# One token-tile pipeline of a Mamba layer and a key-routed expert layer: 25 instead of 21 gathered rows per tile weighed by way of TensorE, and another order of stages and row groups

## What is computed

```python
x = layernorm(x + mamba(x))                      # layer 1
h = silu(x @ W_up.T + b_up) @ W_down.T + b_down  # [tokens, 256]
sim = h @ W_q.T ... keys                         # 2 x 8 heads x 64 keys
sc, indices = top8 of the 64 sums of the top8 of each half, per head
de, ue = down_embed[indices], up_embed[indices]  # 64 rows of 256 and of 512 per token
z = silu(einsum('btd,bthkd->bthk', h, de) * softmax(sc))
x = layernorm(x + einsum('bthk,bthkd->btd', z, ue))
```

## Time and profile before

| | |
|---|---|
| time, median of 3 runs | 3131.76 us (3126.43 to 3133.64) |
| the profiled execution's own time | 3120.3 us |
| its span from the first to the last instruction | 3118.5 us |
| granted TensorE clock, mean over the span | 0.931 |
| busy share DVE / PE / ACT / POOL | 89% / 84% / 75% / 66% |
| mean rate of the DMA engines over the span | 275 GB/s |

### The profile page before, as it was taken

One profiled execution on the slowest core, in us unless ns is written; L12 is line 12 of the kernel. 1 busy time (PEld: TensorE's weight loads), 2 busy tenths in 40 slices (PEclk: granted clock), 3 DMA queues, 4 the chain that ended last, 5 costly groups with the idle time before them and its releaser, 6 DMA issues.

```text
span 3118.5 us, 42958 instructions
## 1 busy us (share of the span) xinstructions
PE 2628.5 (84%) x10688; PEld 1613.2 (52%) x10688; DVE 2770.7 (89%) x10160; ACT 2325.9 (75%) x6674; POOL 2062.9 (66%) x2056
## 2 busy tenths in 40 slices
PE   7988888888888888888888888889888888888862
PEld 4455555555555555555555555555555555555531
DVE  3489899989999999999999999999999998999986
ACT  3477887777887777787777788777788777788753
POOL 0067676666676676676667667667667666667676
PEclk9999999999999999999999999999999999999975
DMA  8078888888888888888888888888888888888897
GB/s 284 26 264 279 283 285 268 280 291 279 279 289 273 273 299 280 281 289 269 268 296 281 281 285 282 263 281 294 282 279 289 272 275 292 279 278 290 271 310 271
DMA packets 189850, 856.65 MB, mean 275 GB/s; under 512 B 36192, under 2 KB 39392, under 8 KB 189088
## 3 DMA queue, kind: packets, MB, share of 16 engines
q0 software_dynamic: 163840, 805.44, 77.0%
q1 hardware_dynamic: 19104, 34.87, 3.2%
q10 hardware_dynamic: 6656, 13.60, 1.2%
HBM read 845.38 MB, written 8.39 MB: 274 GB/s over the span
## 4 chain that ended last, share of the span: by engine, by line
DVE 35%; PE 33%; ACT 11%; issue 9%; DMA 6%; POOL 6%; POOLq 0%; ACTq 0%; DVEq 0%; SPq 0%
PE bank L463 15%; DVE ring L1167 9%; DVE bank L1181 9%; PE bank L479 7%; POOL ring L275 6%; DMA ring<-embed,idx 6%; PE bank L338 3%; DVE i L1097 3%; ACT xc L704 3%; DVE v L1091 2%; DVE xdt L1138 2%; ACT scaled L673 2%; PE bank L470 2%; ACT coef L664 2%; DVE place L1124 1%
## 5 line engine op out<-in xcount | busy, mean ns | idle before, releaser
L275 POOL DMA_INDIRECT ring<-embed,idx x2048 | 2061.6, 1007 | 1040.9 <-issue 517.0
L1181 DVE SCALAR_TENSOR_TENSOR bank<-ring,coef,bank 128x512 f32<-128x512 f32 x1312 | 988.0, 753 | 8.8 <-ACT coef L664 1.4
L1167 DVE SCALAR_TENSOR_TENSOR ring<-ring,hcur 128x256 f32<-128x256 f32 x2048 | 815.4, 420 | 58.0 <-DMA ring<-embed,idx 55.7
L664 ACT ACTIVATE coef<-prob,zp 128x1 f32<-128x1 f32 x2048 | 455.6, 293 | 237.0 <-DVE ring L1167 235.8
L463 PE MATMUL bank<-w_up,zs 128*128 128x512 f32 x1024 | 509.4, 650 | 97.5 <-ACT zs L793 93.9
L506 PE MATMUL bank<-cst,scaled 128*128 128x128 f32 x2688 | 410.9, 305 | 171.9 <-ACT scaled L673 171.8
L506 PEld LDWEIGHTS bank<-cst,scaled 128*128 128x128 f32 x2688 | 351.2, 159 | 245.9 <-ACT scaled L673 213.3
L673 ACT ACTIVATE scaled<-ring,coef 128x512 f32<-128x512 f32 x672 | 446.8, 714 | 10.4
L463 PEld LDWEIGHTS bank<-w_up,zs 128*128 128x128 f32 x1024 | 206.6, 210 | 335.4 <-issue 233.9
L1012 DVE SCALAR_TENSOR_TENSOR xc<-raw,taps,xc 128x128 f32<-128x128 f32 x960 | 265.5, 348 | 90.7 <-ACT xc L704 90.6
L338 PE MATMUL bank<-w_in,ut 128*128 128x512 f32 (+1 forms) x768 | 289.7, 528 | 47.1 <-ACT seg L689 47.1
(11 more groups left out here) (150 smaller groups left out, 3764.4 us busy)
## 6 DMA issues: line engine op xcount, KB each, us to landing
ring<-embed,idx POOLq DMA_INDIRECT x2048, 4.6
ring<-uT SPq DMA_DIRECT2D x4, 2048.0 KB, 14.3
ut<-uT SPq DMA_DIRECT2D x32, 256.0 KB, 6.7
zs<-u SPq DMA_DIRECT2D x32, 256.0 KB, 6.2
out<-acc SPq DMA_DIRECT2D x32, 256.0 KB, 5.0
w_up<-W_upT ACTq DMA_DIRECT2D x1, 4096.0 KB, 12.8
w_in<-W_in ACTq DMA_DIRECT2D x1, 2560.0 KB, 17.2
w_in<-W_in ACTq DMA_DIRECT2D x1, 2048.0 KB, 21.7
```

The costliest lines, as they stand in the source:

```text
L275: pool.indirect_dma_start(out=ring[:, k % RING, :], out_offset=None, in_=embed, in_offset=bass.IndirectOffsetOnAxis(ap=idx[:, half, k:k + ...
L664: m = act.activation(coef[:, k:k + 1], prob_v[:, k:k + 1], ACT.Silu, scale=zp[:, k:k + 1])
L1167: m = dve.scalar_tensor_tensor(out=ring[:, k % RING, 0:DP], in0=ring[:, k % RING, 0:DP], scalar=1.0, in1=hcur[:, :], op0=ALU.mult, op1=ALU ...
L1181: dve.scalar_tensor_tensor(out=total if n == len(DVE_ROWS) - 1 else running[:, :], in0=ring[:, k % RING, DP:ROW], scalar=coef[:, k:k + 1], ...
```

## The change

It rewrites the table `GROUPS` (still 22 groups and 64 rows, now 25 P and 39 D instead of 21 and 43) and the order of the calls in the `tile` functions of PE, ACT and DVE. In ACT `gates` is split into `gate(i, first, b)`, and `skip_term`, which now stands between the two gates, gets one more wait (`hist_ok`, for a copy that reads the buffer it overwrites). No instruction form is new. From the diff, cut:

```diff
@@ -56,7 +56,7 @@
 EPS = 1e-5
 BANK = 512
 BUFS = 4
-GROUPS = ("DD", "PPPD", "DD", "DDD", "PPD", "DDD", "DD", "DDD", "PDDD", "DDD", "DDD", "DDDD", "PDD", "PPPD", "PP", "PDD", "PPPP", "D", "DDD", "PPPD", "D", "PDD")
+GROUPS = ("PPD", "PDD", "PD", "DD", "PPDDDD", "D", "PD", "PDDD", "PDDD", "DDD", "DDD", "DDD", "PDD", "PPPP", "PPPD", "PD", "PP", "PDD", "P", "PPDD", "PD", "DDD")
 NEW = 4
 LAG = 2
 NGRP = len(GROUPS)
...
             def skip_term(i):
 
                 act.wait_ge(xc_ok, i + 1)
+                act.wait_ge(hist_ok, i + 1)
                 for c in range(KX):
                     m = act.activation(xskip[:, c, :], xc[:, c, :], ACT.Copy, scale=dcol[:, c:c + 1])
...
@@ -843,72 +846,73 @@
                     for g in which:
                         coefs(i, g)
 
+                save_x1(i, first)
+                if ahead:
+                    xbc_copy(i + 1, 0)
                 old(4)
                 if ahead:
-                    xbc_copy(i + 1, 0)
                     xbc_copy(i + 1, 1)
+                    inputs(i + 1, 0)
                     xbc_copy(i + 1, 2)
-                    inputs(i + 1, 0)
-                old(5)
-                if ahead:
                     inputs(i + 1, 1)
                 turn_x1(i)
+                old(5)
+                if ahead:
+                    inputs(i + 1, 2)
                 old(6)
-                if ahead:
-                    inputs(i + 1, 2)
-                save_x1(i, first)
+                up_copy(i, 0)
                 old(7)
-                up_copy(i, 0)
-                old(8)
                 up_copy(i, 1)
+                old(8, 9)
                 up_silu(i, 0)
                 up_copy(i, 2)
                 up_silu(i, 1)
-                old(9)
                 up_copy(i, 3)
                 up_silu(i, 2)
-                old(10)
                 up_silu(i, 3)
-                old(11, 12)
+                old(10, 11, 12)
                 turn_h(i)
                 if ahead:
                     masked_steps(i + 1, range(0, NH // 4), False)
                     masked_steps(i + 1, range(NH // 4, NH // 2), False)
+                    conv_silu(i + 1)
                     masked_steps(i + 1, range(NH // 2, 3 * NH // 4), False)
                 old(13)
                 if ahead:
-                    conv_silu(i + 1)
+                    gate(i + 1, False, 0)
                     masked_steps(i + 1, range(3 * NH // 4, NH), False)
-                    gates(i + 1, False)
-                old(14, 15)
+                    skip_term(i + 1)
+                old(14)
+                if ahead:
+                    gate(i + 1, False, 1)
+                old(15)
                 if ahead:
                     decays(i + 1, False)
                 soft_exp(i)
-                if ahead:
-                    skip_term(i + 1)
-                old(16, 17)
+                old(16, 17, 18)
                 if ahead:
                     end_decay(i + 1, range(NH // 2))
-                old(18, 19)
+                old(19)
                 if ahead:
                     end_decay(i + 1, range(NH // 2, NH))
+                    state_decay(i + 1, range(NH // 2))
                 old(20, 21)
-                hand_over(i, first)
-                if ahead:
-                    state_decay(i + 1, range(NH // 2))
+                if ahead:
                     state_decay(i + 1, range(NH // 2, NH))
                     turn_y(i + 1)
+                hand_over(i, first)
                 if not first:
                     sum_out(i - 1)
-                new(0, 1)
                 if ahead:
                     gated_squares(i + 1)
+                new(0)
+                if ahead:
                     gated_rms(i + 1)
-                new(2)
+                new(1, 2)
+                if ahead:
+                    deviation(i + 1)
                 if not first:
                     back_sqrt(i - 1)
-                if ahead:
-                    deviation(i + 1)
                 new(3)
 
...
```

More of the change, by code:

```diff
@@ L534, in tile @@
                     turn_xbc(i + 1, False, 2)
+                old(4)
                 turn_x1(i)
-                old(4, 5, 6)
                 up_proj(i, 0, first, ahead)
@@ L539, in tile @@
                 turn_up(i, 0)
+                old(5)
                 up_proj(i, 2, first, ahead)
+                old(6)
                 turn_up(i, 1)
-                old(7, 8)
+                old(7, 8, 9)
                 up_proj(i, 3, first, ahead)
@@ L546, in tile @@
                 turn_up(i, 3)
-                old(9)
                 down_proj(i, 1, first, ahead)
-                old(10)
                 down_proj(i, 2, first, ahead)
                 down_proj(i, 3, first, ahead)
+                old(10, 11)
                 turn_h(i, ahead)
-                old(11, 12)
+                old(12)
                 key_scores(i, 0)
@@ L558, in tile @@
                     z_proj(i + 1, 1)
-                old(13)
+                    step_sums(i + 1, 0)
+                old(13, 14)
                 if ahead:
-                    step_sums(i + 1, 0)
                     step_sums(i + 1, 1)
@@ L564, in tile @@
                     step_sums(i + 1, 3)
+                old(15)
+                if ahead:
                     turn_x(i + 1)
-                old(14, 15)
+                old(16, 17)
                 if ahead:
                     y_off(i + 1, False)
-                old(16, 17)
+                old(18)
                 if ahead:
@@ L728, in masked_steps, with gate @@
                         m.then_inc(am_ok, 1)
[L730 to L736, removed]
+            def gate(i, first, b):
+                act.wait_ge(z_mm, 2 * i + b + 1)
+                if b == 0 and not first:
+                    act.wait_ge(sim_mm, 2 * i)
+                act.activation(zs[:, b * BANK:(b + 1) * BANK], bank[Z_BANKS[b]][:, :], ACT.Silu).then_inc(z_ok, 1)
             def decays(i, first):
@@ L919, in _ @@
             conv_silu(0)
-            gates(0, True)
+            gate(0, True, 0)
+            gate(0, True, 1)
             act.dma_start(w_up[:, :, :], W_upT.rearrange("(k p) n -> p k n", p=P)).then_inc(w_up_in, 16)
@@ L1244, in tile @@
                     convolve(i + 1, 1, 0)
-                    time_steps(i + 1)
                 old(8)
@@ L1248, in tile @@
                     convolve(i + 1, 1, 1)
-                old(9, 10)
+                    convolve(i + 1, 1, 2)
+                old(9)
                 if ahead:
-                    convolve(i + 1, 1, 2)
                     convolve(i + 1, 2, 0)
+                old(10, 11)
+                if ahead:
                     convolve(i + 1, 2, 1)
-                old(11, 12)
+                    convolve(i + 1, 2, 2)
+                old(12)
                 private(i, first)
+                if ahead:
+                    time_steps(i + 1)
                 old(13)
-                if ahead:
-                    convolve(i + 1, 2, 2)
                 top_half(i, 0)
@@ L1263, in tile @@
                 top_pairs(i)
+                find_pairs(i)
+                places(i)
                 old(15)
@@ L1266, in tile @@
                 shifted(i)
+                old(16)
                 find_half(i, 1)
-                find_pairs(i)
-                old(16)
-                places(i)
-                old(17)
                 picked(i)
+                old(17, 18)
                 numbers(i)
@@ L1276, in tile @@
                     masked_products(i + 1)
-                old(18, 19, 20, 21)
+                old(19, 20, 21)
                 if ahead:
@@ L1283, in tile @@
                     scan_gate(i + 1, 0)
+                softmax(i, first)
+                if ahead:
                     scan_gate(i + 1, 1)
-                softmax(i, first)
                 if not first:
                     weigh_all(i - 1, NGRP - 1, False)
-                new(0, 1)
+                new(0)
                 if ahead:
                     new_state(i + 1)
-                new(2)
+                new(1)
                 if not first:
                     back_sum(i - 1)
-                new(3)
+                new(2, 3)
                 if ahead:
```

12 lines of the change are left out of this document (4 added, 8 removed).

## The result

The changed kernel takes 3113.2 us (median of 5 runs, 3108.0 to 3114.4) against 3127.7 us of the kernel before beside it. The ratio is 0.9945, 95% interval 0.993 to 0.996: 0.55% faster, where 1.8% were forecast (3075 us). It lies outside the stated range, 3005 to 3112 us, by 1 us. The profiled execution's span is 3106.7 us, before 3118.5.

What follows compares the result with a forecast made beforehand. Half A was taken as bound by a PE and ACT chain, half B by DVE. 92.25 - 1.6 (B) - 0.2 (A) = 90.4 us a tile, 31 x 1.8 = 56 us off 3131.8, rounded to 3075 us; range 3005 to 3112.

Steps and rivals of the forecast that it cites:

- half B: From `private` to DVE's start on the old tile's last D rows: DVE's at 39.9 us, forecast 38.3 us.
- PE has its own part here: In half B PE stands at group 14's P rows until ACT scales them, three `step_sums` behind; wait priced at nothing.
- Half A: From DVE's start on the old tile's last D rows to `private`: set by a PE and ACT chain, 52.3 us, forecast 52.1.
- base case: Whole tile 90.4 us instead of 92.25, with 1.6 us still lost to low clock at `up_proj`; 3075 us, 34%.
- rival 1: PE's clock stays up: Half A falls by 0.2 + 1.6 us, half B as forecast; 3.4 us a tile, 3026 us, 25%.
- The weighed rule: At `up_proj` in Half A: without long PE idle gaps 1.6 us a tile would come back; the forecast kept them lost.
- Four rows off DVE: Four rows per tile go from D to P: 2.6 to 3.2 us less DVE time a tile, 82 us or more if DVE-bound.
- ACT's limit in B: In half B `scan_out` waits for both `end_decay` calls: 33.2 us on ACT, making it later than DVE by 1.3 us.
- DVE's wait for group 10: In Half A DVE waits some 2 us in group 12 for these coefficients, with about 1.5 us in hand at `down_proj`'s end.
- rival 3: Gain mostly given back by ACT rows and gather ring: half B 39.3 or a 1 us gather stall; 3107 us, 15%.
- Rival 4: Slower: `hand_over` on ACT comes late and DVE's new work waits for `hcur`; 3 us beyond gives 3163 us, 8%.
- Rival 5: No change: PE and ACT chains set both halves, so DVE's saved time becomes idle time; 3130 us, 6%.

Runs made afterwards that it cites:

- experiment 4: Changed kernel plus 12 spare matmuls on PE in its 3.39 us idle time ahead of the P rows of group 16: 3068.9 us, ratio 0.9829 to before.
- experiment 9: Changed kernel plus spare matmuls in three PE idle times (12 ahead of group 16's P rows, 8 ahead of `turn_y`, 8 ahead of third `turn_xbc`): 3022.5 us.
- experiment 12: Kernel of experiment 9 with `y_off` ahead of `old(16, 17)` and 7 instead of 12 spare matmuls ahead of it: 3021.2 us, ratio 0.9653 to before.
- experiment 5: Changed kernel with `y_off` moved ahead of `old(16, 17)`, plus 8 spare matmuls ahead of `turn_y`: 3094.7 us, 30 us slower than without the spare work.
- experiment 7: Changed kernel with `y_off` ahead of `old(16, 17)`, plus group 10's coefficients made ahead of the last `up_copy` on ACT: 3075.6 us, ratio 0.9842 to before.
- experiment 6: Changed kernel with `y_off` ahead of `old(16, 17)`, plus `back_sqrt` put back ahead of `deviation` on ACT: 3088.4 us, 24 us slower than without the swap.
- experiment 8: Kernel before plus 12 spare matmuls on PE ahead of its `y_off`: 3123.4 us (10 runs), ratio 0.9985 to before.

## Why the prediction was wrong

**The step that failed** is the one in half B: "PE has its own part here", with its wait priced at nothing. I looked only at the P rows of group 14 and left out that `old(16, 17)` now stands ahead of `y_off`. PE idles 3.39 us there and comes back at low clock. `y_off`, which before was done ahead of that idle time, and `y_diag` then run on the path to `scan_out`, and ACT, which I had as the later one, is done 1.8 us earlier in the long tile. B was 39.8 us, forecast 38.3. With the clock held B is 38.7 (experiments 4, 9, 12), so some 1.2 us of the miss are the clock and 0.4 us my sum of ACT's work.

The base was off too. I took B before as 39.9 us, the mean distance of 92.25 less one tile's A. But the first and the last distance are short (86.8 and 86.4 us), and in the middle tiles B was 40.4 us. Against that the change took 0.5 us off B, where a fall to 38.3 would have been 2.1.

**Half A was right as a number, for a reason half wrong.** Forecast 52.1, measured 52.4 us, no less than the 52.3 of before. I had kept the 1.6 us for `up_proj` at low clock as a constant. It is not: A is 50.4 us when the clock is up and 53.6 us when it is down, and the mean came out near my figure. The base case and rival 1 are not two cases but take turns from tile to tile. That the mean came out near 52.1 is luck.

**The weighed rule.** The Trainium skill, "TensorE: Matmul & The Clock Gate", section "HAM oscillation — how this bites in real kernels", says to keep PE free of long idle gaps. As I applied it, to the gap ahead of `up_proj` alone, it did not come true: that gap shrank from 3.12 to 0.69 us, and `up_proj` still took 9.39 us in the long tile. Applied to the whole tile it was the better guide. With the gaps of 3.39, 1.90 and 1.7 us filled the clock was 1.00 (experiment 9), and two of these are under 2 us. Whether fewer fillings would do was not tried, but for single ones. One filling alone gained 44 us in one kernel (experiment 4) and lost 30 us in another (experiment 5).

**The other steps.** Four rows off DVE: 64 us of busy time less, where I had 82 us from the distances of starts. ACT's limit in B: right in kind, `scan_out` waits for `end_decay`, by 0.5 us a tile at held clock and not 1.3. The 0.6 us ahead of `back_norm`: measured 0.55. `hcur`: DVE waits for it once in the run (2.8 us), as good as nothing, as priced. The convolution's wait: gone. DVE's wait for group 10: there in half of the tiles, 39 us in all, and off the path (experiment 7). The larger one for group 5, 63 us in all, I had not seen. In experiment 9 it is still 1.3 us a tile, with the 0.7 us for `down_proj` behind it. What the wait ahead of `back_norm` costs, experiment 6 left open. Gathers: DVE's wait for them is 49 us in the whole run, 56 before, so nothing, as priced. The time lies near rival 3's 3107 us, but its mechanism, small extra costs on ACT and the ring, is not what the runs show. Rival 4 did not happen. Rival 5 came nearest in kind, though not in size: with PE's chain in both halves, DVE's 64 us less of work took 12 us off the span of the profiled execution. But B was not PE's before (experiment 8). The edge stretches I left as they were: 160.0 us and 96.0 us after, 159.8 and 98.9 before. The 51 us at held clock stand against my 56: the mechanics of the change were priced about right, if partly by luck (B gained 1.8 us and not 1.6, A nothing and not 0.2). That the change would move the low clock into B was not priced.

What stays open: why a given spacing of idle times makes the low clock fall in A, in B, or alternate. Experiment 6 shows that swapping two instructions of 0.3 us on another engine moves it. No run here says by which rule.

## What to carry to other kernels

When a change takes work off the busiest engine, look at which engine the chain then runs through. Once that is TensorE, each of its waits can cost twice, by its length and by the low clock behind it. Read the granted clock and the spacing of single rounds of the loop, not only the means: the mean clock was 0.94 before and after, while rounds of 89.8 and 94.1 us with equal work pointed at the cause. And before a chain is reordered, list for the waiting engine what stands behind each wait: the P rows put ahead of `y_off` cost nothing with the clock held and 49 us without.

## What the runs showed of the hardware

- Work that nobody needs made the kernel 2.9% faster: 28 spare matmuls of 128x112 per tile, 3113.2 to 3022.5 us, with the granted clock at 1.00 instead of 0.94 from 1000 to 2800 us. In the kernel before 38 of them gave 1.8%, and 13 at one place (ahead of `up_proj`) 1.6%.
- TensorE's clock stands at 1.2 or 2.4 GHz. The same four matmuls took 3.59 us in the change and 1.88 us in experiment 4, and 16 of another kind took 9.39 and 7.13 us in neighbouring tiles of one execution.
- With PE's idle time of 3.39 us filled and those of 1.7 and 1.9 us (2.3 there) left, A still ran from 50.6 to 54.2 us at a clock of 0.95 (experiment 4). With all three filled it ran from 50.5 to 50.6 us at 1.00 (experiment 9).
- The same low clock costs nothing or much by where it falls. In half B of the kernel before, which DVE held, a rise from 0.96 to 1.00 left B at 40.4 us (experiment 8). In the change, 0.93 to 1.00 took B from 39.8 to 38.7 us (experiment 4).
- A removed wait or a filled one can lengthen the loop: swapping two roots, which removed a wait of DVE, went with 24 us more (experiment 6), and eight spare matmuls in one wait with 30 us more (experiment 5).
